# One block of sixteen-head attention beside a two-layer local transformer: heads written out, first stage rebuilt

## What is computed

```python
xn = layernorm(x)                          # no gain, no bias
# branch 1: full attention, 16 heads of 16 columns, and a second norm of xn
q, k, v = heads(xn @ W_qkv.T)
attn = softmax(q @ k.T * 16**-0.5 + spatial_bias)   # bias: -0.1*dist/max(dist) on 256x256 points
s = (attn @ v) @ W_proj.T + b_proj + layernorm(xn) * gamma + beta
# branch 2: two layers, 8 heads of 64, window 128, rotary positions, gated feed-forward
g = silu(two_layers(xn))
out = x + s * g
```

## Time and profile before

| what | us |
|---|---|
| median of 3 runs | 3315.66 (3314.2 to 3316.36) |
| profiled execution | 3317.31 |
| its span, first to last instruction | 3315.5 |
| stage 1, to the first maximum tile | 182.0 |
| first maximum tile to the last store of stage 2 | 182.0 to 1684.0 |
| rest | 1684.0 to 3315.5 |

### The profile page before, as it was taken

How to read it: one execution, slowest core, us unless ns; L and a number is a source line. 1 busy time by engine, 2 the same in 40 slices (tenths; PEclk the granted TensorE clock), 3 DMA queues, 4 the chain that set the end, 5 groups by cost and what they waited for, 6 DMA issues and landing times.

```text
span 3315.5 us, 101292 instructions
## 1 busy us (share of the span) xinstructions
PE 3100.0 (94%) x37288; PEld 1998.7 (60%) x37288; DVE 2413.4 (73%) x4643; ACT 2243.5 (68%) x4655; POOL 858.8 (26%) x952
## 2 busy tenths in 40 slices
PE   5779999999999999999969999999999999999998
PEld 3434444444444444444437777777777777777776
DVE  6778888988888888898856566666665665665664
ACT  2358888888888888888846656556556556566564
POOL 3510000000000000000024444434444444444443
PEclk9889999999999999999979999999999999999999
DMA  4541111111111111111120111110101110101110
GB/s 138 177 156 36 44 44 44 44 37 45 44 44 38 41 44 44 48 35 44 44 71 19 32 33 40 38 30 26 35 30 40 38 33 27 34 27 40 38 38 4
DMA packets 154834, 154.40 MB, mean 47 GB/s; under 512 B 15136, under 2 KB 128120, under 8 KB 154488
## 3 DMA queue, kind: packets, MB, share of 16 engines
q1 hardware_dynamic: 154488, 149.50, 13.9%
HBM read 90.73 MB, written 58.72 MB: 45 GB/s over the span
## 4 chain that ended last, share of the span: by engine, by line
PE 82%; issue 6%; ACT 5%; DVE 4%; POOL 2%; SPq 1%; DMA 0%; POOLq 0%; DVEq 0%; ACTq 0%
PE banks L1288 14%; PE banks L1328 13%; PE banks L1345 13%; PE banks L1512 8%; PE banks L1394 7%; PE banks L1524 6%; PE banks L1440 4%; PE banks L1473 4%; PE banks L1483 3%; PE banks L1405 3%; PE banks L1452 3%; DVE pair_max L1007 2%; ACT kT L837 1%; ACT qT L830 1%; ACT vw L824 1%
## 5 line engine op out<-in xcount | busy, mean ns | idle before, releaser
L1007 DVE TENSOR_REDUCE pair_max<-banks 128x1 f32<-128x1024 f32 x1039 | 1261.2, 1224 | 160.3 <-PE banks L1288 108.7
L795 ACT ACTIVATE probs<-banks 128x512 f32<-128x512 f32 x2057 | 1106.6, 601 | 195.0 <-PE banks L1328 160.1
L1288 PE MATMUL banks<-k_aug,q_aug 96*32 96x512 bf16 x8312 | 853.5, 388 | 68.2 <-issue 43.5
L1328 PE MATMUL banks<-q_aug,k_aug 98*32 98x512 bf16 x8228 | 846.3, 387 | 0.0
L1345 PE MATMUL banks<-probs,v_cur 128*32 128x256 f32 x8192 | 639.5, 384 | 0.1
L1288 PEld LDWEIGHTS banks<-k_aug,q_aug 96*32 96x32 bf16 x8312 | 242.2, 97 | 432.5 <-DVE pair_max L1007 213.8
L1512 PE MATMUL banks<-hnT,w_sb 128*114 128x128 f32 x3072 | 365.0, 276 | 0.9 <-ACT hnT L868 0.9
L1328 PEld LDWEIGHTS banks<-q_aug,k_aug 98*32 98x32 bf16 x8228 | 252.1, 97 | 188.2 <-issue 12.8
L1512 PEld LDWEIGHTS banks<-hnT,w_sb 128*114 128x114 f32 x3072 | 346.2, 179 | 22.0 <-ACT hnT L868 22.0
L1345 PEld LDWEIGHTS banks<-probs,v_cur 128*32 128x32 f32 x8192 | 263.6, 111 | 136.4 <-issue 16.1
L624 POOL TENSOR_TENSOR norms<-norms,half_power 128x8 f32<-128x8 f32 x128 | 210.5, 1644 | 442.7 <-DVE norms L1094 442.7
(11 more groups left out here) (141 smaller groups left out, 4071.7 us busy)
## 6 DMA issues: line engine op xcount, KB each, us to landing
acc_scratch<-acc_sb SPq DMA_DIRECT2D x128, 256.0 KB, 2.4
heads_win<-acc_scratch SPq DMA_DIRECT2D x512, 64.0 KB
q_aug<-q_parts SPq DMA_DIRECT2D x34, 192.0 KB, 2.8
k_aug<-k_parts SPq DMA_DIRECT2D x34, 192.0 KB, 2.8
q_parts<-parts SPq DMA_DIRECT2D x48, 128.0 KB
k_parts<-parts SPq DMA_DIRECT2D x48, 128.0 KB
x_in<-in_x SPq DMA_DIRECT2D x10, 512.0 KB, 4.1
q_aug<-q_parts SPq DMA_DIRECT2D x34, 128.0 KB, 2.4
```

The lines of the kernel that those rows point to most:

```text
L795: nc.scalar.activation(probs[:, step % PRING, :], banks[:, (use - first_use) % SRING, :], ACT.Exp, scale=SCALE).then_inc(prob_ready, 1)
L1007: nc.vector.tensor_reduce(pair_max[:, q, half:half + 1], banks[:, 4 + 2 * (t % 2):6 + 2 * (t % 2), :], AX.XY, ALU.max).then_inc(smax_read, 1)
L1288: last = nc.tensor.matmul(banks[m:m + CT, 4 + t % 4, :], q_aug[0:TERM_ROWS, b, q * P + m:q * P + m + CT], k_aug[0:TERM_ROWS, b, kq * BANK: ...
L1328: last = nc.tensor.matmul(banks[m:m + CT, (use - use_of(first_step)) % SRING, :], k_aug[0:AUG, b, kb * P + m:kb * P + m + CT], q_aug[0:AUG ...
```

## The change

In stage 2, PE, ACT and DVE no longer loop over heads: `turns()` runs `for h in range(HEADS)` while the program is built, so that all 16 bodies stand one after the other. The order of the work within a body and the waits of its first three tiles stay. POOL keeps its loop; SP writes head 0 out and loops over the other 15.

In stage 1 `layer_norm` falls into `norm_stats`, `norm_variance` and `norm_apply`, run once for a chunk, two chunks ahead; both norms come from these statistics, since the second norm is xn times `ratio`. `residual` makes xn*ratio*gamma on DVE in one operation for a tile, and POOL only adds beta. PE turns the next chunk between blocks 1 and 2 of q and k. x is loaded first. A parts DMA carries all three parts of a block (4 in a chunk for 12), since the DRAM layout is (head, feature, part, token); each load of `q_aug` and `k_aug` takes 12 DMAs of 64 KB for 6. The loops run over 3 pairs of chunks, the last pair is written out (`chunks`). `q_aug`, `k_aug`, `v_cur` and the small tensors get memory of their own, so batch 0 is loaded during the last chunk, and PE and DVE pass into stage 2 without the common meeting; only ACT waits for `phase1_end`, which SP now signals alone. The distances are worked out in the last two chunks and the first steps of stage 2, and POOL clears `v_cur` and fills k's -1 rows at the very start. The weights of stage 3 are loaded in parts during head 0.

```diff
     xT_dram = nc.dram_tensor("xT_scratch", (2, P, T), F32, kind="Internal").ap()
-    q_dram = nc.dram_tensor("q_parts", (HEADS, PARTS * HD, T), BF16, kind="Internal").ap()
-    k_dram = nc.dram_tensor("k_parts", (HEADS, PARTS * HD, T), BF16, kind="Internal").ap()
+    q_dram = nc.dram_tensor("q_parts", (HEADS, HD, PARTS, T), BF16, kind="Internal").ap()
+    k_dram = nc.dram_tensor("k_parts", (HEADS, HD, PARTS, T), BF16, kind="Internal").ap()
     res_dram = nc.dram_tensor("res_scratch", (T, D), F32, kind="Internal").ap()
...
+        def chunks(engine):
+
+            with engine.Fori(0, NCHUNK // 2 - 1) as it:
+                for u in range(2):
+                    yield it * 2 + u, it, u, True, True
+            for u in range(2):
+                yield NCHUNK - 2 + u, NCHUNK // 2 - 1, u, u == 0, False
...
-        def turns(engine):
+        def turns():
 
             yield 0, range(FIRST_STEP)
-            with engine.Fori(0, HEADS) as h:
+            for h in range(HEADS):
                 yield h, range(FIRST_STEP, FIRST_STEP + STEPS)
...
+            for c, it, u, ahead, ahead2 in chunks(nc.sync):
...
+                sp.wait_ge(xnT_ready, c + 1)
+                nc.sync.sem_inc(xnT_seen, 1)
+                sp.dma_start(xT_dram[:, :, bass.ds(token, CHUNK)].rearrange("k p t -> p k t"),
+                             xnT[:, u]).then_inc(xT_stored[u], 16)
+                for mb in range(NMB):
+                    if mb == 2:
+                        sp.wait_ge(res_ready, c + 1)
+                        sp.dma_start(res_dram[bass.ds(token, CHUNK), :].rearrange("(j p) d -> p j d", p=P),
+                                     xn2[:]).then_inc(res_stored, 16)
+                    sp.wait_ge(part3, c * NMB + (mb + 1))
+                    nc.sync.sem_inc(parts_seen, 1)
+                    sp.dma_start(rows[mb], parts[:, mb]).then_inc(parts_stored[mb], 16)
+                if ahead2:
+                    sp.wait_ge(xn_ready, c + 3)
                     sp.dma_start(x_in[:, u], xv[bass.ds(after_next, 1)][0]).then_inc(x_loaded[u], 16)
...
+                elif ahead:
...
+                        sp.wait_ge(parts_stored[mb], 16 * (NCHUNK - 1))
+                    load_aug(0, 0)
             for mb in range(NMB):
-                sp.wait_ge(parts_stored[mb], 16 * PARTS * (NCHUNK + 1))
+                sp.wait_ge(parts_stored[mb], 16 * (NCHUNK + 1))
+            load_aug(0, 1)
...
             nc.sync.sem_inc(phase1_end, 1)
 
-            sp.wait_ge(phase1_end, 5)
...
             nc.gpsimd.memset(v_cur[:, :, :, HD:VW], 1.0).then_inc(v_copied, 1)
             pool.wait_ge(v_copied, 2)
+            nc.gpsimd.memset(k_aug[TERM_ROWS:AUG], -1.0).then_inc(minus_set, 1)
...
+            for c, it, u, ahead, ahead2 in chunks(nc.gpsimd):
+                for mb in range(NMB):
+                    if mb == 1:
+                        pool.wait_ge(res_step, 1)
+                        pool.wait_ge(xn2_ready, c + 1)
+                        nc.gpsimd.tensor_tensor(xn2[:], xn2[:], beta_sb[:].unsqueeze(1).to_broadcast([P, JT, D]),
+                                                ALU.add).then_inc(res_ready, 1)
+                    pool.wait_ge(part2, c * NMB + (mb + 1))
+                    nc.gpsimd.tensor_tensor(parts[:, mb, 2 if mb < 2 else 0], rest[:, mb], parts[:, mb, 1],
+                                            ALU.subtract).then_inc(part3, 1)
+                if not ahead2 and not ahead:
+                    pool.wait_ge(dist_red, 1)
+                    nc.gpsimd.partition_all_reduce(dmax[:, 1:2], dmax[:, 0:1], P, RMAX).then_inc(dist_red, 1)
+            pool.wait_ge(v_copied, 2)
             pool.wait_ge(v_saved, NCHUNK + 1)
-            pool.wait_ge(bias_ready, 1)
...
-            with nc.scalar.Fori(0, NCHUNK // 2) as it:
-                for u in range(2):
-                    c = it * 2 + u
-                    for mb in range(NMB):
-                        if mb == 0:
-                            root(c + 1, 0)
-
-                        act.wait_ge(parts_stored[mb], c * (16 * PARTS) + 16 * PARTS)
-                        act.wait_ge(qk_done, c * NMB + (mb + 1))
-                        nc.scalar.copy(parts[:, mb, 0 if mb < 2 else 2], banks[:, 2 + mb, :]).then_inc(part1, 1)
-                        act.wait_ge(rest_ready, (c + 1) * NMB + (mb + 1))
-                        nc.scalar.copy(parts[:, mb, 1], rest[:, mb]).then_inc(part2, 1)
-                    root(c, 1)
+            root(1, 1)
+            for c, it, u, ahead, ahead2 in chunks(nc.scalar):
+                first_part(c, 0)
+                first_part(c, 1)
+                second_part(c, 0)
+                if ahead:
 
                     act.wait_ge(xT_stored[1 - u], it * 16 + (16 + 16 * u))
                     act.wait_ge(v_done, c + 1)
                     keep_xT(c + 1, 1 - u)
-                    act.wait_ge(v_done, c + 2)
-                    nc.scalar.copy(v_all[:, bass.ds(it * (2 * JT) + u * JT, JT), :],
-                                   banks[:, 6:8, :].rearrange("p a (j d) -> p (a j) d", d=D)).then_inc(v_saved, 1)
-            act.wait_ge(v_saved, NCHUNK + 1)
-            nc.scalar.sem_inc(phase1_end, 1)
-            act.wait_ge(phase1_end, 5)
-            act.wait_ge(dist_scale, 1)
-            nc.scalar.activation(bias_exp[:], dist[:], ACT.Exp, scale=dmax[:, 4:5]).then_inc(dist_exp, 1)
+                if not ahead:
+                    act.wait_ge(dist_step, 5)
+                    nc.scalar.activation(dist[:], dist[:], ACT.Sqrt).then_inc(dist_sqrt, 1)
+                second_part(c, 1)
+                first_part(c, 2)
+                first_part(c, 3)
+                second_part(c, 2)
+                if ahead2:
+                    root(c + 2, u)
+                second_part(c, 3)
+                act.wait_ge(v_done, c + 2)
+                nc.scalar.copy(v_all[:, bass.ds(c * JT, JT), :],
+                               banks[:, 6:8, :].rearrange("p a (j d) -> p (a j) d", d=D)).then_inc(v_saved, 1)
+            act.wait_ge(phase1_end, 1)
...
-            for h, steps in turns(nc.scalar):
+            act.wait_ge(dist_scale, 1)
+            nc.scalar.activation(bias_exp[:], dist[:], ACT.Exp, scale=dmax[:, 4:5]).then_inc(dist_exp, 1)
+            for h, steps in turns():
...
+                dve.wait_ge(ln_sqrt, c + 1)
+                nc.vector.reciprocal(rstd[:, u], roots[:, u]).then_inc(ln_step, 1)
+                dve.wait_ge(ln_step, c * LN_STEPS + 5)
+                nc.vector.tensor_tensor(ratio[:, u], roots[:, u, 0], rstd[:, u, 1], ALU.mult).then_inc(ln_step, 1)
+                for j in range(JT):
+                    last = nc.vector.tensor_scalar(xn[:, u, j, :], x_in[:, u, j, :], mean[:, u, j:j + 1],
+                                                   rstd[:, u, 0, j:j + 1], ALU.subtract, ALU.mult)
+                last.then_inc(xn_ready, 1)
+
+            def residual(c, u):
+
+                dve.wait_ge(res_stored, c * 16 + 16)
+                dve.wait_ge(ln_step, c * LN_STEPS + 6)
+                dve.wait_ge(xn_ready, c + 1)
+                for j in range(JT):
+                    last = nc.vector.scalar_tensor_tensor(xn2[:, j, :], xn[:, u, j, :], ratio[:, u, j:j + 1],
+                                                          gamma_sb[:], ALU.mult, ALU.mult)
+                last.then_inc(xn2_ready, 1)
...
+            for c, it, u, ahead, ahead2 in chunks(nc.vector):
+                split_rest(c, 0)
+                residual(c, u)
+                if not ahead:
+                    dve.wait_ge(dist_step, 3)
+                    nc.vector.tensor_tensor(dist[:], dist[:], dtmp[:], ALU.add).then_inc(dist_step, 2)
+                split_rest(c, 1)
+                if ahead2:
+                    dve.wait_ge(x_loaded[u], it * 16 + 32)
+                    norm_stats(c + 2, u)
+                split_rest(c, 2)
+                if ahead2:
+                    norm_variance(c + 2, u)
+                if not ahead:
+                    dve.wait_ge(dist_sqrt, 1)
+                    nc.vector.tensor_reduce(dmax[:, 0:1], dist[:], AX.XY, ALU.max).then_inc(dist_red, 1)
+                split_rest(c, 3)
+                if ahead2:
+                    dve.wait_ge(xT_done, c + 1)
+                    norm_apply(c + 2, u)
+                elif ahead:
+                    dve.wait_ge(dist_in, 16 * 5)
+                    for kb in range(3):
+                        nc.vector.tensor_scalar(dist[:, kb, :], crow[:, 0, :], ccol[:, kb, 0:1], None, ALU.subtract)
+                        last = nc.vector.tensor_scalar(dtmp[:, kb, :], crow[:, 1, :], ccol[:, kb, 1:2], None,
+                                                       ALU.subtract)
+                    last.then_inc(dist_step, 1)
+                    dve.wait_ge(dist_step, 1)
+                    nc.vector.tensor_tensor(dist[:], dist[:], dist[:], ALU.mult).then_inc(dist_step, 1)
+                    nc.vector.tensor_tensor(dtmp[:], dtmp[:], dtmp[:], ALU.mult).then_inc(dist_step, 1)
...
```

(22 more changed lines are left out.)

333 lines of the change are left out of this document (154 added, 179 removed).

## The result

The changed kernel takes 3198.47 us (median of 4 runs, 3197.72 to 3199.55) against 3316.01 for the kernel before in the same comparison: a ratio of 0.9646, 95% interval 0.9629 to 0.9662, so 117.5 us less. I had forecast 3180, with a range of 3165 to 3208. The time lies inside the range, 18 us above the forecast, and outside the 8 us on either side of it to which I had given half of the chance.

The account below looks back on a forecast made before the run. PE, busy 94% of the span, was taken as the bound, with gains only where it idles or runs slow. Profiled 3317.31 less 66 (heads), less 70.4 (stage 1), plus 0.7 gives 3181.6, as median 3180 us; range 3165 to 3208.

Parts of the forecast that it names:

- rival 1: Stage 1: the chain through DVE and POOL still sets it, 14.5 us a chunk, 3197 in all; chance 0.22.
- the case that I had given 0.07: A joint or the end of stage 1 costs 15 to 30 us more; chance 0.07.
- the signs named: Waits on nothing gone, 88.5 us head to head, stage 1 chunks 12 us, PE's longest wait there under 1 us.
- Stage 1, start: Start to first q block: 13.1 us for 26.65, bounds 11.5 to 16, with x first in SP's queue.
- Stage 1, chunks: First chunk 14.5 us, six at 12.0, last 12.0; first maximum tile at 111.6 for 182.00, 70.4 saved.
- The jumps: Stage 2's fifteen joints between heads: 4.9 us excess each goes except 0.5; 66 us saved, bounds 56 to 74.
- rivals 2 and 3: Stage 2 heads: the wait is not the jump's, 3246, chance 0.04; or straight code starves PE, 3670, chance 0.02.
- Rival 3: Heads written out: fetching straight code starves PE, at least 296 instructions a packet, 490 us lost, 3670; chance 0.02.
- the term of the joint: Between heads in stage 2: new scores wait for all earlier exponentials, a 0.5 us stall, bounds 0 to 1.2.
- The register operations: Loop register operations removed from the heads: taken at nothing, since PE is busy 10.95 of 10.99 us.
- The way into stage 2: First maximum tile to first exponential, 15.5 us before: 0.7 us added for ACT's later bias.
- The loads' twelve DMAs and stage 3's weights: Stage 2: 12 DMAs for 6 per q_aug and k_aug load, stage 3's weights loaded during head 0; both cost nothing.

Follow-up runs that it names:

- e8: The kernel after with one more POOL product of 2.35 us in each chunk of stage 1, which nothing waits for; 3215.08 us.
- e1: The kernel after with POOL's products of batch 0 put ahead of its wait for attn@v and its copies of v; 3169.62 us.
- e4: e1 plus one tiny POOL addition that needs nothing, directly behind the all-reduce of the largest distance; 3161.09 us.
- e5: The kernel after with the loops over heads put back on PE, ACT and DVE, so stage 1's change alone; 3293.58 us.
- e10: e5 with 24 semaphore increments on PE ahead of the loop, which shift its body by 24 instructions; 3294.68 us, one run.
- e6: The kernel before with heads written out on PE, ACT and DVE and POOL's products ahead of its copies; 3233.52 us.
- e2: The kernel before with the heads written out on PE, ACT and DVE and nothing else changed; 3259.44 us.
- e9: The kernel before with only PE's heads written out, ACT and DVE keeping their loops; 3285.62 us.

## Why the forecast was right, and where it was off

The time fell into the range, but not by the forecast's account. The range reached up to 3208 for rival 1 (3190 to 3205), whose mechanism does not set the time here; 3198 matches its 3197 by luck. What came is the case that I had given 0.07, a joint that costs 15 to 30 us more. Of the signs named, the waits on nothing are gone, but head to head is 89.5 us for the 88.5 named, and stage 2 gained 44.2 us where under 50 was to mean that the forecast is wrong (50.5 if only the 15 heads are counted). So the forecast is right for stage 1 and the jumps' idle time, and wrong for what stands at the joint.

- **Stage 1, start**: forecast 13.1, measured 12.55. Right; x landed as said, and DVE's norm began at 4.95 for 5.4.
- **Stage 1, chunks**: 14.5 for the first (measured 14.36), six of 12.0 (11.43 once steady, 69.9 in all), 12.0 for the last (13.76: PE waits 3.28 for ACT's copy of v, where 1.0 to 1.5 were put). Two small misses of opposite sign, 111.6 against 110.56. The reason given was half right. The busy sum of 8.5 us for DVE left out the holds; its real figure is 11.28. The Trainium skill, "SBUF — State Buffer", "SBUF: two separate sides", has the exclusion as a rule, and the trace agrees (0.15 us operations lasting 1.1 and, in `e8`, 2.35). The rival had this mechanism, and `e8` shows it as the next limit, 0.3 us behind PE; it did not decide here. PE's longest wait at the stage's end, 3.28 us, is also above the 1 us named.
- **The jumps**: the waits on nothing are gone, as said, and rivals 2 and 3 fell: no wait at even distances, 212 instruction packets for 252. Rival 3's count of at least 296 instructions a packet took each executed instruction as fetched anew; the same sum on the kernel after gives 352 with packets of the same 16.4 KB (3.47 MB/212, 4.13 MB/252), so it does not measure a packet. What failed is the term of the joint, 0.5 us: it looked at ACT's exponentials and not at POOL, whose wait for the last attn@v and 2.07 us of products stood hidden under the jump. The joint costs 13.3 less 10.88, 2.4 us, of which some 0.3 are the clock's fall at 3 of 15 joints; 15 times the difference to 0.5 is 29 us. `e1` puts it back to 0.46.
- **The register operations**, taken at nothing since PE is full: PE was full at 10.95 of 10.99, but with DVE's straight code the same 120 groups are 0.11 shorter, 13 us in all. That this gain hid nearly half of the loss above is luck; the forecast for the heads is off by what is left of the two, 15.5 us.
- **The way into stage 2**: 0.7 put for ACT's bias. ACT needed even less (15.2 us from maximum tile to exponential, 15.5 before), but POOL's late product behind the reduction had no term, and the stretch came out 5.6 longer than forecast. `e4` gives it back: head 0's last store is at 218.45 for 226.62 in `e1`. In the kernel before that reduction stood far from stage 2's start.
- **The loads' twelve DMAs and stage 3's weights**: nothing, as said.

Of the range's bounds for the heads, 56 to 74, the measured 50.5 lies outside, because the bounds too priced only ACT's restart.

## What to carry to other kernels

An idle time that is removed uncovers what ran under it: before a jump or wait is priced, list what every other engine does in that window and where its queue stands, POOL's copies and waits too. In a queue, put what is ready early ahead of what waits late; here the order of POOL's two kinds of work is worth nothing with the jump and 29 us without. Where one engine's operations are held by another's, as DVE's by POOL's in the earlier trace rows, add the holds to the busy sum, and test the margin by giving the hidden engine a little more to do. A forecast whose parts miss in opposite directions can land in its range; check it part by part.

## What was not expected of the hardware

- A jump costs PE 2.4 to 4.2 us idle at its target, 2.8 to 3.1 on average in each run with loops. With the target 17 matmuls (`e5`) or 5 (`e10`) ahead of a fixed place of the stream it stops another 1.7 or 2.3 us on average in the middle of a batch. Shifting the body by 48 instructions was worth 37 us of 3294, so what stands ahead of a loop can move this kernel's time by 1% by its mere length.
- POOL's first product after a partition all-reduce starts 6.8 us (`e4`) and 7.1 us (kernel before) after it, or some 8 us after what it waits for (kernel after); another 5.8 to 6.9 us on nothing stand before the reduction in the kernel after and the runs built on it. A copy in between (117.80) does not take the delay away, a tiny product does.
- PE's granted clock fell at 14 or 15 of the 15 joints with a jump (0.89 or lower in the stretch), at 2 to 9 of 15 where PE waits up to 1.9 us for POOL, and at none in `e1`, `e4` and `e6`, where it does not wait. A fall makes a joint 1.3 to 1.5 us longer (`e2`, `e9`, kernel after).
- In this kernel DVE's loop form costs 0.11 us in a group of 11 us although DVE has 0.8 us idle in it; ACT's costs nothing that shows.
